# Layer-0 cross attention: the order of key, output and query matmuls on TensorE, and of queries and residual on VectorE

## The reference

```python
def _L0_xattn_ref(queries, keys, values, boxes, Wq, bq, Wk, bk, Wv, bv, Wo, bo, Wg, bg):
    ...
    emb = box_relational_embedding(boxes)
    g = jax.nn.relu(jnp.einsum('bnmd,hd->bhnm', emb, Wg) + bg[None, :, None, None])
    q = (queries @ Wq.T + bq).reshape(b, nq, H, D_K).transpose(0, 2, 1, 3)
    k = (keys @ Wk.T + bk).reshape(b, nk, H, D_K).transpose(0, 2, 1, 3)
    v = (values @ Wv.T + bv).reshape(b, nk, H, D_V).transpose(0, 2, 1, 3)
    a = jnp.einsum('bhqd,bhkd->bhqk', q, k) / jnp.sqrt(jnp.float32(D_K))
    mn = jax.nn.softmax(jnp.log(jnp.clip(g, 1e-06, None)) + a, axis=-1)
    out = jnp.einsum('bhqk,bhkd->bqhd', mn, v).reshape(b, nq, H * D_V)
    return out @ Wo.T + bo
...
    x = x + _L0_attn_ref(_layernorm(x, axis=-1), ...)
    x = x + _L0_xattn_ref(_layernorm(x, axis=-1), ctx_1024, ctx_1024, fside_BxSx4_0, ...)
    x = x + _L0_ffn_ref(_layernorm(x, axis=-1), ...)
    ...
```

## Time and profile before

| what | value |
|---|---|
| median of three runs | 481.63 us (478.5 to 483.13) |
| profiled execution | 481.88 us |
| its span, first to last instruction | 480.1 us |
| TensorE matmul busy | 320.3 us, 67% of the span |
| VectorE busy | 335.9 us, 70% |
| ScalarE busy | 194.4 us, 40% |
| chain that ended last, TensorE's share | 36% |
| chain that ended last, VectorE's share | 19% |

### The profile page before, as it was taken

The page is one execution under the profiler, slowest core; times in us unless marked ns, Lnnn a source line. Parts: engine busy times, 40 slices in busy tenths (PEclk is TensorE's granted clock), DMA queues, the critical chain, the costliest instruction groups (busy, mean ns, idle before and its releaser), DMA issues.

```text
span 480.1 us, 8901 instructions
## 1 busy us (share of the span) xinstructions
PE 320.3 (67%) x3651; PEld 197.5 (41%) x3651; DVE 335.9 (70%) x479; ACT 194.4 (40%) x310; POOL 90.0 (19%) x86
## 2 busy tenths in 40 slices
PE   2605779767666575799999973920095998789821
PEld 0201233222222334477777761400033777467710
DVE  0796899999999955666666644488833674666574
ACT  1519968546445330122222252475113442434420
POOL 0070033444343403400000000000003341112000
PEclk9856799888899597699999996765576798989965
DMA  8600000000005768100000000000000000000001
GB/s 236 255 0 16 1 1 22 23 22 22 1 21 101 132 117 286 73 3 1 3 1 3 3 1 0 0 0 1 0 0 0 3 4 3 1 2 5 3 0 44
DMA packets 22500, 16.91 MB, mean 35 GB/s; under 512 B 17216, under 2 KB 20416, under 8 KB 22336
## 3 DMA queue, kind: packets, MB, share of 16 engines
q1 hardware_dynamic: 22464, 16.39, 12.5%
HBM read 11.67 MB, written 4.72 MB: 34 GB/s over the span
## 4 chain that ended last, share of the span: by engine, by line
PE 36%; DVE 19%; SPq 6%; issue 5%; ACT 3%; DMA 1%; POOL 0%; DVEq 0%; ACTq 0%; POOLq 0%
PE psum L441 29%; SPq L423 6%; PE psum L699 3%; DVE small L1455 2%; DVE arena_a L1397 2%; PE psum L581 2%; PE psum L548 2%; DVE small L1539 1%; DVE arena_a L1417 1%; ACT arena_b L1050 1%; DMA g_scratch<-arena_a 1%; DVE arena_b L1510 1%; DVE arena_b L1516 1%; DVE arena_b L1543 1%; DVE xc L1220 1%
## 5 line engine op out<-in xcount | busy, mean ns | idle before, releaser
L441 PE MATMUL psum<-arena_b 64*64 64x9 f32 (+2 forms) x1348 | 75.3, 278 | 43.8 <-DVE arena_b L1364 30.6
L441 PEld LDWEIGHTS psum<-arena_b 64*64 64x64 f32 (+2 forms) x1348 | 34.9, 141 | 73.6 <-issue 38.8
L441 PE MATMUL psum<-arena_a 64*64 64x64 f32 (+2 forms) x1056 | 34.8, 235 | 9.0 <-ACT arena_a L904 5.4
L1539 DVE TENSOR_REDUCE small<-psum 128x16 f32<-128x1024 f32 x16 | 19.6, 1225 | 20.2 <-PE psum L441 20.2
L441 PEld LDWEIGHTS psum<-arena_a 64*64 64x64 f32 (+1 forms) x1056 | 21.9, 139 | 28.5 <-issue 15.8
L1148 POOL TENSOR_TENSOR arena_b<-arena_b 128x512 f32<-128x512 f32 x16 | 24.8, 1551 | 43.3 <-DVE arena_b L1334 43.3
L441 PE MATMUL psum<-arena_a,xw 128*128 128x128 f32 x256 | 31.1, 279 | 2.4 <-ACT arena_a L969 2.2
L441 PEld LDWEIGHTS psum<-arena_a,xw 128*128 128x128 f32 x256 | 30.1, 195 | 4.0 <-ACT arena_a L969 2.7
L441 PE MATMUL psum<-arena_b,const 32*128 32x128 f32 (+1 forms) x138 | 9.1, 346 | 32.3 <-DVE arena_b L1462 32.0
L1172 POOL MEMSET arena_b<- 128x16 f32 x4 | 0.3, 128 | 160.1 <-DVE x L1529 160.1
L1145 POOL TENSOR_TENSOR arena_b<-arena_b 128x512 f32<-128x512 f32 x16 | 21.9, 1369 | 44.0 <-DVE arena_b L1351 44.0
(11 more groups left out here) (218 smaller groups left out, 731.1 us busy)
## 6 DMA issues: line engine op xcount, KB each, us to landing
g_scratch<-arena_a SPq DMA_DIRECT2D x16, 256.0 KB, 6.6
logg<-g_scratch SPq DMA_DIRECT2D x1, 3584.0 KB, 13.2
xw<-in_xw SPq DMA_DIRECT2D x1, 2048.0 KB, 9.1
arena_b<-in_rkvo SPq DMA_DIRECT2D x8, 192.0 KB, 2.3
ffn_w<-in_ffn SPq DMA_DIRECT2D x1, 576.0 KB, 10.8
x<-in_xT SPq DMA_DIRECT2D x2, 256.0 KB, 3.0
arena_a<-in_boxes SPq DMA_DIRECT2D x8, 64.0 KB, 4.0
arena_b<-in_rkvo SPq DMA_DIRECT2D x8, 64.0 KB, 1.9
```

The source lines that it names most:

```text
L441: return nc.tensor.matmul(o, l, r, start=start, stop=stop, **kw)
L1539: v_.tensor_reduce(mx.rearrange("p (r h) -> p r h", r=4), s4, axis=AX.X, op=ALU.max).then_inc(s.a_max, 1)
```

## The change

On TensorE the next tile's keys (`x_k`) go ahead of the output transposes, and the next queries (`x_q`) ahead of the output projection (`x_wo`). On VectorE the copy of the next queries goes ahead of the previous tile's residual. Nothing else differs.

```diff
--- before.py
+++ after.py
@@ -564,16 +564,16 @@
                             last = mm(half(pA, sl)[64 * b:64 * b + 64, cc * S:(cc + 1) * S], q_x[u][r, cc, tok],
                                       k_x[u][r, cc, tok])
                 last.then_inc(s.s_psum, 1)
-                if prev:
-                    x_out_transposed(t - 1, 1 - u)
                 if nxt:
                     pe.wait_ge(s.vx_done, 2 * t + 2)
                     x_k(t + 1, 1 - u)
                 if prev:
-                    x_wo(t - 1, 1 - u)
+                    x_out_transposed(t - 1, 1 - u)
                 if nxt:
                     pe.wait_ge(s.s_scaled, t + 1)
                     x_q(t + 1)
+                if prev:
+                    x_wo(t - 1, 1 - u)
                 pe.wait_ge(s.s_done, t + 1)
                 if prev:
                     pe.wait_ge(s.ot_done, t)
@@ -1419,10 +1419,10 @@
                     x_keys(t + 1, 1 - u)
                 if not prev:
                     dve.wait_ge(s.g_in, 16)
+                if nxt:
+                    x_queries(t + 1, 1 - u)
                 if prev:
                     x_residual(t - 1)
-                if nxt:
-                    x_queries(t + 1, 1 - u)
 
             dve.wait_ge(s.x1_done, 2)
             ln_centre(1, 1)
```

## The result

The changed kernel takes 473.73 us (median of 6 executions, 472.65 to 475.66) against 480.40 us of the kernel before on the same occasion (median of 6, 478.5 to 483.13). The ratio is 0.986, with a 95% interval of 0.9818 to 0.9902, so the changed kernel takes 1.4% less time and the interval excludes no change.

A forecast was written before the change was run, and what follows sets the result against it. TensorE was taken to bound the layer-0 cross-attention loop, with one wait a tile for VectorE. Six tiles at 0.89 us give 5.3 us off: 476.6 from the profiled 481.88, 476.3 from the median 481.63; range 473.5 to 479.7.

The forecast's parts named there:

- What bounds the loop: Layer-0 cross attention: TensorE sets the pace, idling only in six waits of L548 for L1397, 4.7 us in all.
- x_k closes the gap: Tiles 1 to 6: x_k starts 0.03 us after the last score weight load, gaining 0.89 us a tile.
- The rest keeps its length: TensorE's four reordered groups in a tile take 6.30 us start to start, against 6.29 before.
- lower bound of 4.7: Least gain over six tiles, 6 x 0.78 us, if only the gap between matmul rows can be closed.
- upper bound of 0.98: Most gain in us a tile, 5.9 in all, if x_k starts at 225.93, the last score row being pipeline tail.
- The margins: TensorE's groups in the new order: every input is ready before its group starts, by 0.57 us (x_wo) at least.
- Part 3: VectorE copies the next queries ahead of the residual: no cost or gain, product still has 1.86 us margin.
- Rival (a): The wait moves in part, likeliest to x_wo: 0.4 us a tile lost again, 478.7 us; chance 0.09.
- Rival (b): The change does nothing, as x_k cannot start earlier in the loop: 481.6 us; chance 0.03.
- Rival (c): Clock at FFN matmuls behind the loop rises later: 485.5 us, chance 0.03; opposite, both groups warm: 471.0, chance 0.05.
- the line of 1%: Whole kernel: about 1%, 4.8 us, is what a measurement can tell from no change.

The follow-up runs named there:

- the first run: Only the next keys moved ahead of the output transposes, all else as in the kernel before: median 485.12 us against 481.44, ratio 1.005.

## Why the prediction was right, point by point

- **What bounds the loop.** TensorE with one wait a tile: right. With the wait gone, TensorE is busy for 11.19 of 11.19 us, and the period is the sum of its groups from start to start: product and scores 2.02, the four reordered groups 6.34, L581 0.97 and x_v 1.86. One reading was incomplete: "Nothing else idles TensorE there by more than the 0.17 us" holds for the matmul side. The weight-load side also has six waits of 0.8 us for L975, 4.9 in all, and gaps of up to 0.3. They are the same in the changed kernel, and its matmul side stays busy through them, so nothing hangs on it. And the 0.016 us is the distance of two records of the scores; a matmul is two of them.
- **x_k closes the gap.** Right in kind. The step at which x_k starts was put at 0.03 after the last load and was 0.07.
- **"The rest keeps its length", 6.30 us.** This is the term that was off. The four groups take x_k 1.89, transposes 0.88, x_q 1.78, x_wo 1.79, in all 6.34. The prediction had halved the 3.57 of x_k and x_wo and so gave x_k 1.79; but in a group that starts the chain anew the first matmul starts together with its load (both at 221.34), while in a group that follows another the load leads by 0.11 (223.12 and 223.23), so x_k takes 0.10 more from its matmul start to the next group's. The loads keep their pace: 1.78 from x_k's first to the next group's. The transposes, no longer behind a wait, take 0.05 less. With the hand-over this makes 0.81 a tile in place of 0.89, and 4.85 in place of 5.3, close to the lower bound of 4.7. The upper bound of 0.98 did not come about: x_k's load starts 0.07 after the last score load has ended, and not ahead of its matmul.
- **The margins.** All held, and were nearly as worked out: x_k 0.77 (0.73 predicted), transposes 1.09 (0.95), x_q 0.83 (0.75), x_wo 0.55 (0.57), product 0.74 (0.74). The first three are wider since the queue from x_k on runs 0.03 to 0.13 us later behind L1393 than forecast.
- **Part 3, VectorE's order costs and gives nothing.** Right, both ways: 12.00 with it alone, 11.20 without it.
- **Rival (a)** did not come, but the run with the doubled copy shows that its margin was 0.51, and that a copy 0.92 later costs 0.51 a tile. The prediction said that x_q stands where x_k had covered the copy; what this cover is worth the first run shows: without it the period is 12.57.
- **Rival (b)** did not come. **Rival (c)**: the two groups behind the loop ran at 0.76 and 0.71 as before at 0.76 and 0.70, and took 10.74 and 8.82 us where they took 10.85 and 8.90. From its start to VectorE's step behind it (L1466) the first of them took 10.5 to 10.9 us in the three profiles of before and 10.1 to 10.8 in those of the changed kernel. The time behind the loop does scatter by about 3 us (194.0 to 197.1), but in both kernels alike (before 194.0 to 197.0, changed 194.7 to 197.1). The clock has a part in it: from 380 to 450 us the first profile of before has a granted clock of 0.96 and 0.94, and the same stretches of the second, which is 3 us shorter behind the loop, have 1.00. That fits what the Trainium skill (TensorE: Matmul & The Clock Gate, Part 1) says of a rise that is not tied to the kernel's start.
- **The time.** 476.3 was forecast with a range of 473.5 to 479.7; 473.73 and later 475.63 were measured. The mechanism's part, 4.85, is below the forecast's 5.3, and the first measured difference, 6.7, above it. By the loop alone the first comparison would have had 480.40 - 4.85 = 475.55; that 473.73 came out, 0.2 us inside the lower end of the range, is owed to what lies outside the loop, and not to the mechanism. The forecast of 1.1% lay near the line of 1%, and so did the loop's true share.

## What to carry to other kernels

When an engine stands at a wait with ready work behind it, the work to pull ahead is one whose input is long there, and the group that is moved back must not lose the cover of its own producer: here the keys could go first only because the queries took their place between the transposes and the projection. Write down for each group in the new order when its input is ready and when the group starts; the smallest of these margins says what the next wait would be and how much change it bears. A gain of 1% is better read from the period in one trace, which repeats to 0.02 us, than from times that scatter by a per cent.

## What the runs showed of the hardware

- A TensorE group of 16 records of 128x128 takes 1.78 to 1.79 us from its start to the next group's when it follows on another 128x128 group, and 1.89 when it starts behind a wait or behind 64x64 pieces (x_k at 221.34, and x_wo in the run with the doubled copy, at 227.81). The weight loads are 1.78 apart in both cases (221.34 to 223.12, 227.81 to 229.59); what is missing in the second is the lead of 0.11 that the load otherwise has over its matmul.
- Two ScalarE copies of 128x1024 back to back start 0.92 us apart, though each is 1.02 us long.
- TensorE's eight x_v records of tile 0 took 3.68 us at 1.2 GHz, 2.57 with the rise in their midst and 1.94 at 2.4 GHz. How far the rise has come by then changes between executions of one kernel (2.57, 3.68 and 2.43 us in the changed kernel), and is worth up to 1.4 us in tile 0 (14.65 to 16.05).
